# A hybrid block of gated delta-rule attention, state-space scan and FP4 FFN on one core: order of ACT's work in a slot, a second place for turned rows, shorter rings, and matmuls without a consumer in two waits' places

## The reference

```
x = x + attn_a(ln(x))     # delta rule, 32 heads of 128, q and k shared by two heads
x = x + ffn(ln(x))        # FP4 weights, one scale per 128 inputs
x = x + attn_b(ln(x))     # state-space scan, 16 states per channel
x = x + ffn(ln(x))        # same weights
```

```
state = state * exp(g_t);  delta = (v_t - k_t @ state) * beta_t
state = state + outer(k_t, delta);  out_t = q_t @ state
```

## Time and profile before

| | |
|---|---|
| time, median of 3 runs | 4253.48 us (4252.47 to 4253.96) |
| the profiled execution: time, span | 4257.75 us, 4256.0 us |
| busy: PE, DVE, ACT, POOL | 4116.7, 3411.5, 2318.2, 464.1 us |
| mean granted clock of PE | 0.986 of full |
| attention ends, block border | about 3025 us |
| slots of the third block begin | 3189 us |
| scans | 3220 to 4083 us |
| last down matmul of run 7 ends | about 4249 us |

### The profile page before, as it was taken

One profiled execution on the slowest core, in us unless ns is written; L12 is line 12 of the kernel. 1 busy time (PEld: TensorE's weight loads), 2 busy tenths in 40 slices (PEclk: granted clock), 3 DMA queues, 4 the chain that ended last, 5 costly groups with the idle time before them and its releaser, 6 DMA issues. The chain is left out here.

```text
span 4256.0 us, 83003 instructions
## 1 busy us (share of the span) xinstructions
PE 4116.7 (97%) x30773; PEld 2524.4 (59%) x30773; DVE 3411.5 (80%) x8712; ACT 2318.2 (54%) x5479; POOL 464.1 (11%) x470
## 2 busy tenths in 40 slices
PE   7899999999999999999999999998899999989999
PEld 4566666666666666666666666666444444444444
DVE  5888888888888888888888888886547989898940
ACT  3555555555555555555555555554445655565543
POOL 1111111111112111112111111110000000000000
PEclk9999999999999999999999999998899999999999
DMA  2111111111011112211111111110104545444520
GB/s 76 42 34 36 39 38 37 33 38 39 31 43 34 31 43 73 58 44 34 32 38 39 34 41 34 37 37 6 67 1 136 160 138 173 154 153 144 174 67 10
DMA packets 202470, 263.52 MB, mean 62 GB/s; under 512 B 18223, under 2 KB 101427, under 8 KB 202067
## 3 DMA queue, kind: packets, MB, share of 16 engines
q1 hardware_dynamic: 202066, 258.20, 19.2%
HBM read 249.24 MB, written 8.91 MB: 61 GB/s over the span
## 5 line engine op out<-in xcount | busy, mean ns | idle before, releaser
L518 PE MATMUL bank<-x_blocks,w_qkv 128*128 128x512 f32 x2048 | 930.4, 597 | 4.9 <-ACT raw L812 4.2
L518 PEld LDWEIGHTS bank<-x_blocks,w_qkv 128*128 128x128 f32 x2048 | 376.5, 193 | 396.5 <-issue 377.7
L1135 DVE SCALAR_TENSOR_TENSOR conv<-raw,conv_w,conv 128x1024 f32<-128x1024 f32 x384 | 516.1, 1344 | 66.2 <-ACT conv L786 57.0
L600 PE MATMUL bank<-w_z_unit,x_blocks 128*128 128x256 f32 x2048 | 491.7, 384 | 0.0
L644 PE MATMUL bank<-w_out_unit,oT 128*128 128x512 f32 x1008 | 486.8, 605 | 0.3 <-ACT oT L838 0.3
L600 PEld LDWEIGHTS bank<-w_z_unit,x_blocks 128*128 128x128 f32 x2048 | 374.4, 193 | 41.5 <-issue 0.2
L1385 PE MATMUL bank<-xnT_f,w_gu 128*128 128x512 f32 x704 | 329.2, 612 | 9.1 <-ACT xnT_f L1875 8.2
L812 ACT COPY raw<-bank 128x512 f32<-128x512 f32 x256 | 149.1, 582 | 328.6 <-PE bank L518 328.5
L1403 PE MATMUL bank<-w_down,hidden 128*128 128x512 f32 x704 | 318.0, 595 | 2.8 <-DVE hidden L1425 2.8
L1393 PE MATMUL bank<-xnT_f,w_gu 128*128 128x512 f32 x704 | 316.8, 593 | 0.6 <-DVE hidden L1425 0.5
L916 ACT ACTIVATE k_scaled<-o 128x128 f32<-128x128 f32 x512 | 154.0, 302 | 246.4 <-DVE o L1190 206.6
(11 more groups left out here) (246 smaller groups left out, 7805.8 us busy)
## 6 DMA issues: line engine op xcount, KB each, us to landing
rows_b<-bc_rows SPq DMA_DIRECT2D x256, 256.0 KB, 3.4
rows_c<-bc_rows SPq DMA_DIRECT2D x256, 256.0 KB, 3.5
w_qkv<-in_w_qkv SPq DMA_DIRECT2D x128, 256.0 KB, 2.9
decay<-gc_rows SPq DMA_DIRECT2D x64, 512.0 KB, 3.9
w_z_unit<-in_w_z SPq DMA_DIRECT2D x32, 512.0 KB, 4.3
w_out_unit<-in_w_out SPq DMA_DIRECT2D x32, 512.0 KB, 5.0
x_after<-x SPq DMA_DIRECT2D x16, 256.0 KB, 2.0
x_blocks<-x_after SPq DMA_DIRECT2D x4, 1024.0 KB, 10.7
```

Source lines behind the costliest of these rows:

```text
L518: made = e.matmul(PROJ[:, :], w_qkv[:, p % 2, j, :], xnT[:, n // HK, j, h * BANK:(h + 1) * BANK], start=j == 0, stop=j == KT - 1)
L600: made = e.matmul(ZB[:, i * REP * P:(i + 1) * REP * P], xnT[:, N // HK, j, t * P:(t + 1) * P], w_z[:, N % 2, j, :], start=j == 0, stop=j = ...
L1135: e.scalar_tensor_tensor(acc, raw[:, i % 2, tap:tap + T], conv_w[:, tap, col:col + 1], acc, ALU.mult, ALU.add).then_inc(on["conv"], 1)
```

## The change

1. In the first unit of attention, and ahead of four jobs at the border, PE gets matmuls of 128x512 whose result nobody reads (`keep_streaming`): 8, 5, 2, 7, 7 in the unit and 3, 4, 1, 2 at the border, each just ahead of a wait.
2. In a slot, ACT makes its carry and its decay first, ahead of evictions; the decay ring has 3 places, so a decay waits for the scan of the slot before.
3. `xnT_f` has two places, used by even and odd runs. A run's turns go one per slot, through one bank, at 5 to 2 slots ahead of its start; an eviction waits for the up matmuls of the run two before. The statistics of a run come tile by tile over four slots, and a slot earlier.
4. The `gate` tile is gone: ACT's silu goes to `hidden` and DVE multiplies there in place. The drive ring has 6 places, `SUM_LAG` is 3, and the starts of the runs are others.
5. In the border block the statistics of run 1 come a tile earlier, its rows are normalised in the last two tiles, and two of them are turned inside the last tile.

```diff
@@ attention, tensor
+            def keep_streaming(unit, count):
+                if unit == 0:
+                    for _ in range(count):
+                        e.matmul(OB[:, :], c["ident"][:, :], xnT[:, 0, 0, 0:BANK], start=True, stop=True)
             def g_pair(n, a, pair):
                 N = n
+                if pair == 1 and a == 0:
+                    keep_streaming(N, 8)
...
                 e.wait_ge(on["silu"], 4 * N + V0 + r + 1)
+                if group % 2 == 1:
+                    keep_streaming(N, 4 // group + 1)
...
+                if (level, part) in ((0, 0), (2, 1)) and a == 0:
+                    keep_streaming(N, 7)
@@ tables
-RUN_START = {1: 0, 2: 43, 3: 91, 4: 136, 5: 183, 6: 230, 7: 279}
-SUM_LAG, DRIVE_RING, H_RING = 4, 8, 3
+RUN_START = {1: 0, 2: 46, 3: 92, 4: 136, 5: 184, 6: 235, 7: 281}
+SUM_LAG, DRIVE_RING, H_RING, DECAY_RING = 3, 6, 3, 3
-        uses += [(at - 4 + t // 2, 1, ("ffn_turn", R, t)) for t in range(TILES)]
+        uses += [(at - 5 + t, 1, ("ffn_turn", R, t)) for t in range(TILES)]
@@ second_half
-        xnT, xn = sb("xnT_f", [P, KT, BANK]), sb("xn_f", [P, 2, D])
+        xnT, xn = sb("xnT_f", [P, 2, KT, BANK]), sb("xn_f", [P, 2, D])
@@ silu_gate, make_hidden
-            if U > 0:
-                e.wait_ge(on["hidden"], U)
-            e.activation(gate[:, :], GB[:, :], ACT.Silu).then_inc(on["gate_silu"], 1)
+            if U >= 2:
+                e.wait_ge(on["down_pe"], U - 1)
+            e.activation(hidden[:, U % 2, :], GB[:, :], ACT.Silu).then_inc(on["gate_silu"], 1)
...
-            e.tensor_tensor(hidden[:, U % 2, :], UB[:, :], gate[:, :], ALU.mult).then_inc(on["hidden"], 1)
+            row = hidden[:, U % 2, :]
+            e.tensor_tensor(row, UB[:, :], row, ALU.mult).then_inc(on["hidden"], 1)
@@ border block, tensor
+                e.wait_ge(early["x_early0"], 16)
                 for use in prep[:prep_at[("piece", 1)] + 1]:
+                    keep_streaming({("scale", 0): 3, ("turn0", 0): 4, ("turn0", 2): 1, ("piece", 1): 2}.get(use, 0))
                     prepare(use)
...
                     e.wait_ge(on["prep_read"], prep_at[("piece", 2 * i + 1)] + 1)
+                    for t in range(2):
+                        if i == IT - 1:
+                            prepare(("turn1", t))
@@ border block, scalar and vector
-                    if i == IT - 2:
+                    if i == IT - 3:
                         ffn_rstd(e, 1)
...
-                    if i == IT - 3:
+                    if i == IT - 4:
                         ffn_stats(e, 1)
-                for t in range(TILES):
-                    e.wait_ge(on["prep_made"], prep_at[("turn0", t + 2) if t < 2 else ("turn1", t - 2)] + 1)
-                    ffn_normed(e, 1, t)
+                    for t in range(TILES):
+                        if i == (IT - 3 if t < 2 else IT - 2):
+                            e.wait_ge(on["prep_made"], prep_at[("turn0", t + 2) if t < 2 else ("turn1", t - 2)] + 1)
+                            ffn_normed(e, 1, t)
@@ third block
-        stats_slot = {at - 8: R for R, at in RUN_START.items()}
+        stats_slot = {at - 9: R for R, at in RUN_START.items()}
...
                 if kind == "ffn_turn":
-                    e.copy(xnT[:, :, i * P:(i + 1) * P], split(turn_bank(i))).then_inc(on["work_read"], 1)
+                    e.wait_ge(on["up_pe"], IT * (q - 1))
+                    e.copy(xnT[:, q % 2, :, i * P:(i + 1) * P], split(WB)).then_inc(on["work_read"], 1)
@@ third block, scalar, at the head of a slot (both pieces stood further down before)
+                at = step_of(p - 2)
+                if at is not None and at[0] % NH < NH - 1:
+                    q, i, n = at
+                    e.wait_ge(on["scan"], p - 1)
+                    e.copy(carry[:, n, i:i + 1], h_all[:, (p - 2) % H_RING, BANK - 1:BANK]).then_inc(on["carry"], 1)
+                at = step_of(p + 2)
+                if at is not None:
+                    q, i, n = at
+                    if n == 0:
+                        e.wait_ge(on["dtx"], KT * q + i + 1)
+                    if p + 2 >= DECAY_RING:
+                        e.wait_ge(on["scan"], p + 3 - DECAY_RING)
+                    e.activation(step_decay[:, (p + 2) % DECAY_RING, :], dt[:, (KT * q + i) % 2, :], ACT.Exp,
+                                 scale=rate[:, i, n:n + 1]).then_inc(on["step_decay"], 1)
                 for use in uses_in(slot - 1, 1):
                     evict(use)
```

More of the change, by code:

```diff
@@ L1365, in second_half @@
         x = early["x"]
-        xnT, xn = sb("xnT_f", [P, KT, BANK]), sb("xn_f", [P, 2, D])
+        xnT, xn = sb("xnT_f", [P, 2, KT, BANK]), sb("xn_f", [P, 2, D])
         six, moments, rstd = sb("six_f", [P, TILES, 6]), sb("moments_f", [P, TILES, 2]), sb("rstd_f", [P, TILES])
         shift, shift_ss = sb("shift_f", [P, TILES]), sb("shift_ss", [P, TILES])
-        gate, hidden = sb("gate", [P, BANK]), sb("hidden", [P, 2, BANK])
+        hidden = sb("hidden", [P, 2, BANK])
         squares, rms = sb("squares_f", [P, D]), sb("rms", [P, TILES])
@@ L1384, in gate_mm @@
             for j in range(KT):
-                made = e.matmul(GB[:, :], w_gu[:, j, i * P:(i + 1) * P], xnT[:, j, :], start=j == 0, stop=j == KT - 1)
+                made = e.matmul(GB[:, :], w_gu[:, j, i * P:(i + 1) * P], xnT[:, R % 2, j, :], start=j == 0,
+                                stop=j == KT - 1)
             made.then_inc(on["gate_pe"], 1)
@@ L1600, in prepare, with keep_streaming @@
                     made.then_inc(on["prep_made"], 1)
+                def keep_streaming(count):
+                    for _ in range(count):
+                        e.matmul(GB[:, :], c["ident"][:, :], x[:, 0, 0, :], start=True, stop=True)
+                e.wait_ge(early["x_early0"], 16)
                 for use in prep[:prep_at[("piece", 1)] + 1]:
+                    keep_streaming({("scale", 0): 3, ("turn0", 0): 4, ("turn0", 2): 1, ("piece", 1): 2}.get(use, 0))
                     prepare(use)
@@ L1619, in tensor @@
                         down_mm(e, 0, i - 1)
-                for t in range(TILES):
+                for t in range(2, TILES):
                     prepare(("turn1", t))
-                    if t == 0:
-                        down_mm(e, 0, IT - 1)
+                down_mm(e, 0, IT - 1)
             def scalar(e):
@@ L1809, in work @@
                 last_out = kind == "out" and q == BLOCKS - 1
-                if last_out and i > 0 or kind == "ffn_turn" and i > 0:
+                if last_out and i > 0:
                     e.wait_ge(on["work_read"], k - 1)
@@ L2083, in vector @@
                     add_residual(e, residual_slot[slot])
-                if slot in stats_slot:
+                for t in range(TILES):
+                    R = stats_slot.get(slot + TILES - 1 - t, 0)
+                    if 1 < R < len(RUNS) - 1:
+                        tile_stats(e, R, t)
+                if slot in stats_slot and stats_slot[slot] < len(RUNS) - 1:
+                    all_moments(e, stats_slot[slot])
+                elif slot in stats_slot:
                     ffn_stats(e, stats_slot[slot])
```

43 lines of the change are left out of this document (14 added, 29 removed).

## The result

The changed kernel takes 4264.06 us (median of 10 executions, 4262.48 to 4264.70), the kernel before 4253.72 (10 executions, 4250.90 to 4257.66): ratio 1.0026, 95% interval 1.0018 to 1.0034. It is slower by 10.3 us, 0.24%, a little more than the 8.5 us that the prediction takes as measurable. The range (4230 to 4270) holds the time. The likeliest case, 4254 and no change, did not come; 4264 also lies above that case's own range (4246 to 4262).

What follows compares the result with a forecast made beforehand. PE, busy 97% of the span, was taken to bound the kernel. Scans +2.6, first unit -3.1 and border +1.4 gave +0.9: 4258.7 us as profiled, 4254 as median (chance 0.40), range 4230 to 4270.

Steps and rivals of the forecast that it cites:

- First unit: First attention unit: added matmuls fill PE's waits and keep the clock up, -3.1 us; bounds +4.7 and -4.5.
- Border: Border block between attention and scans: added matmuls +1, moved statistics +1, moved turns -0.6, in all +1.4 us.
- The gaps: Scans, from each FFN run's last down matmul to the next run's first gate: changed starts cost +11.8 us in all.
- run 6: Sixth FFN run's start in the scans: gate 17.2 us after the last down matmul instead of 8.0, +9.2, less 1.3.
- run 5: Fifth FFN run's start in the scans: gate 13.8 us after the last down matmul instead of 8.6, +5.2.
- the sum around run 2: Second FFN run's start: gap 12.2 us instead of 0.4, partly won back earlier: +5.3, and +1.5 for half clock.
- run 7: Seventh FFN run's start in the scans: gap 5.3 us instead of 9.9, and 2 us of clock back, -6.5.
- Waits on ACT: Scans: PE's waits on y go and half of that for hidden, -9.2 us (7.7 and 1.5).
- A: Rival, scans: DVE's chain rather than PE sets the pace, so ending carry stalls gives -22, 4232 us; chance 0.33.
- B: Rival, scans: empty slots cost in full, PE waits for DVE, 4269 us; chance 0.27 with C's bad end.
- C: Rival, first attention unit: fills do nothing, the clock falls as before, +4.7 instead of -3.1, 4262 us; no separate chance.
- A rule on the clock: Scan gaps: transposes do not count as busy for PE's clock; were that wrong, run 6 would be 3 us cheaper.

Runs made afterwards that it cites:

- h1: The kernel before with only ACT's carry and decay moved to the head of the slot (decay ring stays 4): 4246.03 us, ratio 0.9986.
- e3: The kernel before with the changed run starts alone, one of them a slot sooner than in the change: 4258.89 us, ratio 1.0017.
- m1: The changed kernel without its ten added matmuls at the border; the moved statistics and turns stay moved: 4262.19 us, ratio 1.0020.
- h4: The kernel before with ACT's carry and decay at the slot's head and sums three slots behind instead of four: 4237.50 us, ratio 0.9964.
- f1: The changed kernel with run starts like those of before, two of them a slot later than before: 4250.40 us, ratio 0.9995.
- h3: The changed kernel with ACT's decay and carry back behind the evictions, as before: 4273.22 us, ratio 1.0042.
- f4: The changed kernel with the border block as before: no added matmuls there, statistics and turns not moved: 4263.01 us, ratio 1.0024.

## Why the prediction was right or wrong

**Bounds and views.** That DVE's waits for carries would not come back as time, since PE sets the pace: right, and shown by h1 (35.8 us away, 6.6 won).

**First unit (-3.1).** Half right. The five waits are filled and the clock is at full, as said; the gain is 1.5 to 2 us by the medians of 14 profiles. The trace pair alone shows 5.3, but attention of unchanged code ends within a span of 5 us. That PE is never idle afterwards is not so: from 2830 to 3000 us it is busy 147 of 170 us at a granted clock of 0.92 before and of 0.94 in e3, and from 2823 us to the end of attention before took 202.2 us, e3 199.3.

**Border (+1.4).** The size came out near (197.2 against 195.0, +2.2), and its main cause is one of those priced: three fills at half clock (5.1 us predicted, 5.46 measured). The +1 for the moved statistics was wrong; m1 shows none.

**The gaps.** T to gate was within 0.7 us of the measured in five runs and 1.3 short in run 6 (residual of run 5 ending at T+7.7, not T+6.4, since it stood behind DVE's slot rather than behind the squares). The step that failed most is the sum around run 2: I let 6.5 us of the 11.8 come back ahead of T, by the silu wait of 2.06, 1.7 of clock, four turns and a slot of DVE's delay. T came 3.2 us earlier behind the first scan (110.6 instead of 113.8): the wait for the silu went, and one for `hidden` took its place ahead of the same down matmul:

```profile
3324.11 3.70 PE L1417 MATMUL bank<-w_down,hidden 128*128 128x512 f32 x8 [2.07 <-DVE hidden L1438]
```

With the gate's clock run 2 is +10.3 instead of +6.8. Run 6 with its clock is +9.7 (7.9 predicted), run 5 +5.7 (5.2), run 3 -0.9 (-1.6, its gate now at half clock), run 7 -6.2 (-6.5), run 4 -0.4 (0): +18.2 against +11.8.

**Waits on ACT (-9.2).** The rest behind the first scan is 9.5 - 18.2 = -8.7. That it lies near -9.2 is luck. Both causes are real: the shorter lag wins 6.7 us behind the first scan in h4's trace (7.7 priced, for y), and what I had named half of the `hidden` wait, 1.5 us, is the head's effect and larger, 6.7 alone and 9.2 within the change. Added up they are 13.4 us or more, so at least 4.7 were lost again. I had put the rest of the change at nothing, since it "adds no instruction"; the comparison of f1 with h4 shows that this term is not nothing.

**From profile to median.** I took 4.3 us off, since the kernel before was profiled in an execution above its median. The changed kernel's profiled execution is its median, 4264.06. Behind the first scan my terms summed to +2.6 against +9.5; that 6.9, +0.7 at the border and -2.2 in the first unit make the 5.4 by which 4258.7 was short of the profiled 4264.06. The subtraction makes the other 4.3 of the 10 us: the chance in attention's length belonged to that one profile and was not to be carried over to a kernel that had not run.

**Rivals.** A is refuted by h1. B's time, 4269, is 5 us off and C's, 4262, only 2, but neither has the mechanism. Against B: a sum waits for a drive once, 0.9 us, evictions wait for no more than the gaps show, and h3 and h4 show that head and lag gain. B's idea that the tighter coupling costs inside the runs may still be part of what f1 loses against h4. What made the change slower was in the forecast itself, too small by a third. C is out: the clock held.

**A rule on the clock.** The prediction weighed what the Trainium skill states under "TensorE: Matmul & The Clock Gate", Part 4: PE-mode transpose (transposes do not count as busy in the same way). Run 6's gate again starts at half clock, 5.60 us, behind a gap with turns and sums in it. The pauses there, up to 4.16 us, would explain that as well; none of the gaps read here tells the two apart. The prediction also read its row wrongly: the 12.25 busy us of 18 include the gate itself. Between the last down matmul and the gate of run 7 PE is busy 4.3 of 10 us, with turns only and a pause of 4.35 us ahead of them:

```profile
4128.55 1.94 PE L1499 MATMUL bank<-ident,xn_f 128*128 128x128 f32 x8 [4.35 <-ACT xn_f L1924]
```

## What to carry to other kernels

When a table moves work between slots that another engine paces, price each border by the chain that must follow the last use (here square, residual, decay, eviction, once per slot), then test the table alone: here it made 14 us of a change that otherwise came out even. Coming out even does not make the other parts sound. Take such a change apart before judging it: two small edits of it (an order on one engine, one constant) beat both kernels by 16 us and more, and beat the change with the old starts, which contains them, by 13. A wait of 36 us on an engine that does not set the pace was worth 6.6.

## What the runs showed of the hardware

Attention of one and the same code ended between 3020.2 and 3025.3 us in five profiled executions; the granted clock of PE between 2830 and 3000 us was 0.92 in the one and 0.94 in another, and 0.97 or 1.00 in the first 60 us. So single profiles of this kernel compare only to about 5 us, unless they are compared stretch by stretch. A wait of 2.07 us ahead of run 1's last down matmul left the clock up in the change (3.70 us for the four matmuls, granted clock 1.00 over them) and took it down in f4 (0.58 over the first 3.2 us of them):

```profile
3321.77 5.40 PE L1417 MATMUL bank<-w_down,hidden 128*128 128x512 f32 x8 [2.07 <-DVE hidden L1438]
```

After the same wait the four matmuls took 1.7 us more in f4 and m1, the two kernels of the change without the border's fills; whether these are the reason stays open. It is most of the 2.1 us and more that f4 and m1 lost behind the first scan, and so gave back of what they won at the border.
